# Issuing the two token parities of an expert's first-layer product back to back, into four PSUM banks in turn

## The reference

```python
h = (x_flat @ W_gat).reshape(M, HEADS, NUM_EXPERTS)          # graph attention over 262144 edges
...
agg = jax.ops.segment_sum(msg, dst, num_segments=M).reshape(M, HEADS * NUM_EXPERTS) + b_gat
scores = _layernorm(agg, ln_gamma, ln_beta).reshape(M, HEADS, NUM_EXPERTS).mean(1)
topk_s, topk_i = jax.lax.top_k(scores, TOP_K)
w = jax.nn.softmax(topk_s, axis=-1)
for ei in range(NUM_EXPERTS):
    g = jnp.where(topk_i == ei, w, 0.0).sum(-1)
    hh = jax.nn.gelu(x @ W1[ei] + b1[ei], approximate=False)
    out = out + g[..., None] * (hh @ W2[ei] + b2[ei])
```

## Time and profile before

| | |
|---|---|
| median of 3 runs | 1025.7 us (1022.24 to 1026.14) |
| profiled execution, its own time | 1031.22 us |
| its span, first to last instruction | 1029.5 us |
| busy: TensorE matmul / VectorE / ScalarE / GpSimd | 644.5 / 762.1 / 306.7 / 499.9 us |
| mean granted TensorE clock | 0.748 of full speed |

### The profile page before, as it was taken

The page is one execution under the profiler, slowest core; times in us unless marked ns, Lnnn a source line. Parts: engine busy times, 40 slices in busy tenths (PEclk is TensorE's granted clock), DMA queues, the critical chain, the costliest instruction groups (busy, mean ns, idle before and its releaser), DMA issues.

```text
span 1029.5 us, 15298 instructions
## 1 busy us (share of the span) xinstructions
PE 644.5 (63%) x5984; PEld 331.3 (32%) x5984; DVE 762.1 (74%) x1477; ACT 306.7 (30%) x463; POOL 499.9 (49%) x399
## 2 busy tenths in 40 slices
PE   1501472499788888997787969999999410003421
PEld 1200130133333333333333445555656210002421
DVE  3999887697886877667888779998989831008775
ACT  1510350144554645444444431111111010000015
POOL 3990000017676766650000028888888877756000
PEclk9955875556987977669767969999999855555655
DMA  5010004100000000000000222000000000110001
GB/s 152 0 43 6 8 9 99 24 1 1 1 2 1 1 1 0 0 0 0 2 1 1 82 48 53 6 6 7 6 6 7 7 10 10 10 7 1 3 2 41
DMA packets 22001, 17.08 MB, mean 17 GB/s; under 512 B 13488, under 2 KB 18944, under 8 KB 21168
## 3 DMA queue, kind: packets, MB, share of 16 engines
q1 hardware_dynamic: 15424, 14.02, 5.1%
q0 software_dynamic: 5392, 2.18, 2.6%
q10 hardware_dynamic: 1120, 0.00, 0.1%
HBM read 10.51 MB, written 2.54 MB: 13 GB/s over the span
## 4 chain that ended last, share of the span: by engine, by line
PE 41%; DVE 30%; issue 13%; ACT 4%; SPq 2%; another core or an unknown queue 0%; DMA 0%; DVEq 0%; POOL 0%; ACTq 0%; POOLq 0%
PE psum L615 11%; PE psum L748 10%; DVE mx L1259 7%; PE psum L631 4%; DVE arena L1323 3%; PE psum L646 3%; PE psum L739 3%; PE psum L730 3%; SPq L381 2%; DVE arena L1289 2%; PE psum L598 2%; DVE arena L1030 2%; ACT arena L1004 1%; DVE arena L1026 1%; PE psum L669 1%
## 5 line engine op out<-in xcount | busy, mean ns | idle before, releaser
L493 POOL DMA_INDIRECT work<-node_rows,idx x160 | 257.8, 1611 | 53.1 <-issue 48.5
L1259 DVE TENSOR_REDUCE mx<-psum 128x2 f32<-128x512 f32 x256 | 164.3, 683 | 69.8 <-PE psum L631 67.9
L1323 DVE TENSOR_TENSOR arena<-arena 128x4096 bf16<-128x4096 bf16 (+1 forms) x128 | 182.0, 1486 | 18.1 <-PE psum L748 13.9
L915 ACT ACTIVATE arena<-psum 128x1024 f32<-128x1024 f32 x128 | 129.4, 1024 | 158.4 <-PE psum L646 158.4
L615 PE MATMUL psum<-arena 128*32 128x256 f32 x1024 | 168.3, 486 | 2.3 <-DVE arena L1299 1.4
L470 POOL TENSOR_SCALAR work<-arena,cF 128x184 f32<-128x184 f32 x128 | 93.7, 744 | 129.0 <-DVE arena L1159 73.2
L748 PE MATMUL psum<-arena 128*32 128x128 bf16 x2048 | 131.3, 420 | 4.3 <-DVE arena L1323 3.2
L631 PE MATMUL psum<-arena 32*128 32x256 bf16 x512 | 85.5, 340 | 27.5 <-DVE mx L1259 24.5
L748 PEld LDWEIGHTS psum<-arena 128*32 128x32 bf16 x2048 | 78.2, 149 | 43.6 <-DVE arena L1323 11.6
L615 PEld LDWEIGHTS psum<-arena 128*32 128x32 f32 x1024 | 56.8, 130 | 75.6 <-issue 57.8
L461 POOL COPY arena<-arena 128x160 f32<-128x160 f32 x16 | 5.4, 348 | 136.9 <-DVE arena L1145 91.7
(11 more groups left out here) (290 smaller groups left out, 989.7 us busy)
## 6 DMA issues: line engine op xcount, KB each, us to landing
work<-work SPq DMA_DIRECT2D x48, 64.0 KB, 2.0
work<-node_rows,idx POOLq DMA_INDIRECT x160
arena<-in_L_ffn_edge_index_dram SPq DMA_DIRECT2D x2, 1024.0 KB, 10.6
work<-edge_nodes SPq DMA_DIRECT2D x4, 368.0 KB
digits<-arena SPq DMA_DIRECT2D x1, 1024.0 KB, 4.0
arena<-digits SPq DMA_DIRECT2D x1, 1024.0 KB, 4.9
arena<-in_jpat_dram SPq DMA_DIRECT2D x1, 1024.0 KB, 6.8
out_dram<-work SPq DMA_DIRECT2D x4, 256.0 KB, 2.3
```

The costliest lines, as they stand in the source:

```text
L493: pool.indirect_dma_start(gath[:, l, :], None, tab, bass.IndirectOffsetOnAxis(ap=idx[:, l:l + 1], axis=0)).then_inc(done, 16)
L915: act.activation(pbuf[:, m % 4, :, :, :], ps[:, 2 + 2 * (m % 2):4 + 2 * (m % 2), :].rearrange("p j (k q) -> p j k q", k=U), ACT.Exp).then_ ...
L1259: v.reduce_max(mx[:, h, :], ps[:, h % 2, :].rearrange("p (u k) -> p u k", u=U), AX.X).then_inc(mx_done, 1)
L1323: ins = v.tensor_tensor(oh[:, buf, first:first + n, :], hl2[:, s_, bass.ds(blk * HC, HC)].rearrange("p (j c) -> p j c", j=1).broadcast_to( ...
```

## The change

`up` takes an expert instead of a step. It issues the products of both parities one behind the other, into banks 4 * (e % 2) and 4 * (e % 2) + 1 (so 0, 1, 4 and 5 in turn), and waits once for both. The loop calls it for expert 0 and expert 1 ahead of `down(i, 0)`, for expert 2 ahead of `down(i, 2)` and for expert 3 ahead of `down(i, 4)`; ahead of the other `down`s there is no `up`. The GELU reads the new banks. Nothing else is touched, and every line below L730 has a number higher by one.

```diff
-            def up(i, m):
-                e, u, n = m // 2, m % 2, 8 * i + m
-                if m == 0:
+            def up(i, e):
+                n = 8 * i + 2 * e
+                if e == 0:
                     pe.wait_ge(tns_ready, i + 1)
-                    if isinstance(i, int) and i == 0:
+                    if i == 0:
                         pe.wait_ge(hb_done, 2)
-                if m >= 2 or later(i, 0):
-                    pe.wait_ge(hid_done, n - 1)
-                pe.matmul(ps[:, m % 2, :], w1[C * u:C * u + C, e, :], tns[C * u:C * u + C, :],
-                          start=True, stop=True).then_inc(f1_ready, 1)
+                if n >= 4:
+                    pe.wait_ge(hid_done, n - 2)
+                for u in range(U):
+                    pe.matmul(ps[:, 4 * (e % 2) + u, :], w1[C * u:C * u + C, e, :], tns[C * u:C * u + C, :],
+                              start=True, stop=True).then_inc(f1_ready, 1)
...
                 up(i, 0)
                 for m in range(8):
-                    if m < 7:
-                        up(i, m + 1)
+                    if m % 2 == 0 and m < 6:
+                        up(i, m // 2 + 1)
                     down(i, m)
...
-                act.activation(hid[:, m % 4, :], ps[:, m % 2, :], ACT.Gelu, bias=b1c[:, m // 2:m // 2 + 1]).then_inc(hid_done, 1)
+                act.activation(hid[:, m % 4, :], ps[:, 4 * (m // 2 % 2) + m % 2, :], ACT.Gelu, bias=b1c[:, m // 2:m // 2 + 1]).then_inc(hid_done, 1)
```

## The result

Over 20 executions of each kernel the ratio of the changed kernel's time to that of before is 0.990, with a 95% interval of 0.9853 to 0.9947. On 1025.7 us that is 1015.4 (1010.6 to 1020.3); 1018.6 was forecast, a ratio of 0.993. The change makes the kernel about 1% faster. The medians of all the executions (1026.5 after, 1025.3 before) do not show it, for single ones scatter over 30 us, and the ratios leave out those of a slower state, to which the profiled execution of the changed kernel belongs.

The account below looks back on a forecast made before the run. The end was taken to follow GpSimd's gathers, blocked by VectorE: 0.9 us from the stage plus 6.2 from five more quick gathers gave 7.1, so 1024.1 for the profiled execution and a median of 1018.6 us, range 1015 to 1027.

Parts of the forecast that it names:

- The direction and the path: Whole kernel: faster, because the end follows the gathers, not the stage's end; gathers 92 and 160 come 7.1 us sooner.
- The pair at 1.1 us: TensorE in the stage: a second parity on other array rows is free, so a pair takes about 1.1 us.
- The holes of 0.8 that let a gather in: VectorE idles 0.8 us in steps with a pair, each admitting one quick gather; five more in all, worth 6.2 us.
- Stage: -1 us: The stage's length: 1 us shorter, with bounds of +10 and -10.
- The other way to the same sum: All 160 gathers: 64 blocked at 2.80 and 96 free at 1.25 make 299.2 us, where they now take 306.
- The first chunk: Low clock: a pair takes 2.08 us; the second replaces a 0.8 wait, 1.3 later, partly given back by later steps.
- A chunk's start: Between the counts 3.25 us stand where 2.93 stood, so VectorE's hole grows from 1.84 to about 2.2.
- Slack behind the stage: VectorE's merge after the stage: ready at about 825, needed at 834.7, so 9 us of slack, enough.
- The port: Shared by VectorE and GpSimd: a skill rule implied up to 4.7 us on the stage's end; forecast took no cost.
- Rival 1: The gathers don't profit: holes nearer 0.4 than 0.8 admit none, little beyond the stage's 1 us arrives; chance 0.2.
- Rival 2: Pairs don't overlap: stage up to 10 us later, gathers 9 to 10 sooner, kernel 4 to 10 faster; chance 0.1.
- Rival 3: Slower: the slow products after the stage follow TensorE's place in its instructions and may grow, to 1040 us; chance 0.1.

Follow-up runs that it names:

- less: The changed kernel with 150 gathers in place of 160, the last ten slots of every list left unfetched; ratio to the kernel before 0.9719.
- rows: The changed kernel with each pair made of two experts of one parity, so on the same array rows; ratio to the kernel before 0.9849.
- after5: The changed kernel measured again as it was, in five rounds; ratio to the kernel before 0.9895.
- banks: The kernel before, still one product per step, but with the four PSUM banks of the change; ratio to the kernel before 0.9986.
- tiny: The changed kernel with first-layer products over only 8 of the 512 tokens of a chunk; ratio to the kernel before 0.9964.
- hold: The changed kernel with TensorE's 192 small products waiting for the end of all gathers; ratio to the kernel before 0.9884.
- spread: The changed kernel with `down` of steps 2, 4 and 6 moved between the step's two count blocks; ratio to the kernel before 0.9972.
- pause: The changed kernel with GpSimd waiting between gathers 92 and 93 until the small products are done; span's end 433.4 us after the first one-hot instruction, against 412.2.
- split2: The changed kernel with each 4096-element one-hot instruction cut into two of 2048; 1091 us, the shorter of two runs, against 1032.
- split4: The changed kernel with each 4096-element one-hot instruction cut into four of 1024; ratio to the kernel before 1.1324.
- some: The kernel rows with every fourth block's 4096-element one-hot instruction cut into two of 2048; ratio to the kernel before 0.981.

## Why the prediction was right, point by point

**The direction and the path: right.** The last gather came 9.0 us sooner (7.1 forecast), the turn 9.0 and the end 9.1, and less shows that the end hangs on the gathers. TensorE's 10.8 us less of work were not what counted, as rows shows. The 1024.1 us forecast for the profiled execution came out at 1032.3, because its stage began 10.2 us later; the ratio, 0.990 against 0.993, is what the forecast is to be measured by.

**The pair at 1.1 us: right.** 1.13, and 1.98 without the second set of rows.

**The holes of 0.8 that let a gather in: right.** Measured 0.75 to 0.84, one quick gather in each. The count of five more came out as four, one in each chunk, because the first chunk's first hole did not get longer and took three as before: 4 x 1.25 = 5.0 us instead of 6.2. (The four other traces with the same stage have five or six more.) The reading of the hole of 0.52 stands, although the row at 679.36 in the earlier trace rows is cut off by its window: VectorE goes on there with four instructions, of which 2.33 us is the first.

**The stage: the term that was mis-sized.** "Stage: -1 us" was the working; it measured -3.9 (-3.1 in after5). With the gathers' 5.0 that makes 8.9, against 9.0 measured. So the 7.1 is near the 9.0 partly by luck: the stage's part was 3 us too small and the gathers' part 1.2 too large. Over the five traces with this stage and the two with the one before it, the stage gained 3.5 us and the count 5, so it is the stage's term that was off. The other way to the same sum, 64 blocked at 2.80 and 96 free at 1.25, or 299.2 us, came out at 297.2: the numbers 64 and 96 were right, but the gather that starts behind a hole is held only for what is left of VectorE's instruction, and takes 1.90 to 2.18 us instead of 2.50. Cut at the chunks' first holes, the gain is 0.9 in the first chunk (59.09 to 58.22), 1.05 and 1.17 in the next two and 0.8 in the last. Two things failed:

- *The first chunk.* I put a loss of 1.3 us on the second pair, at the low clock. The two pairs did take 3.79 us, where one took 2.08. But the loss was not there: TensorE no longer idled 0.77 us ahead of `down`, and the granted clock came back sooner. Windows that begin 4.0 and 6.0 us after the first one-hot instruction, first of the kernel before, then of the changed one:

```profile
612.16:614.16 2.00, 2.00 (x16) 1.77 (x19) 1.69 (x2) 0.49 (x2) 1.91 (x1) 0.50 0.87 111
614.16:618.16 4.00, 3.57 (x59) 2.30 (x52) 0.25 (x1) 0.00 (x0) 2.87 (x4) 0.71 0.59 130
```

```profile
622.35:624.35 2.00, 2.00 (x18) 1.43 (x20) 1.69 (x2) 0.38 (x2) 1.90 (x1) 0.80 0.91 118
624.35:628.35 4.00, 3.89 (x64) 2.24 (x56) 0.36 (x1) 0.72 (x2) 2.88 (x4) 1.00 0.70 156
```

  In the first window TensorE is at 1.2 GHz before (0.50) and already mostly at 2.4 after (0.80). `down` took 1.24 instead of 1.97, and the first hole came out at 3.96, no longer than the 4.06 of before. after5 shows the same (0.79, 4.01). The other kernels bear it out: where two full pairs stand ahead of the first `down`, the clock rises 4.1 to 5.5 us after the first one-hot instruction; in before, banks and tiny, where TensorE idles ahead of it (0.77 us, in tiny 0.34), at 8.3 to 8.5. The hole itself is less steady: in less it is 3.29 us, in hold 4.77.

- *A chunk's start.* I put two pairs at 1.11 each and a hole of 2.2. Together they take 1.99, the products stand 2.96 between the counts (671.25 to 674.21) where they stood 2.93, and the hole stayed at 1.8. That is the other 0.2 to 0.4 us in each of the two whole chunks behind the first.

**Slack behind the stage: right.** 9 us forecast for VectorE, 9.45 measured. The end did not turn over to another wait.

**The port.** A quick gather under way when VectorE restarts costs it next to nothing in these traces: in rows one begins at 661.73, VectorE at 661.79, and the eight instructions take 11.31 us as elsewhere; the most is the 2.33 us at 679.36 of the earlier trace rows, where such an instruction takes 2.29 elsewhere. So the rule by which each of the five quick gathers would cost VectorE up to 0.94 us did not come true, and the row that I took held. The other way round the blocking is complete: a gather of 0.94 us mostly takes 2.50 beside 4096-element instructions and 1.43 where they are cut to 2048, and one that starts beside a 4096-element instruction ends 0.82 us behind that instruction's end (the first of all 1.06). The Trainium skill (SBUF — State Buffer, "Who interferes with whom") has such a lock for the whole instruction, but infers that a `tensor_tensor` doesn't hold up the making of DMA descriptors; here `tensor_tensor` with both inputs in SBUF did hold up the issue of gathers, so the inference gives the wrong answer for this case. Whether a gather is held at its descriptors or at the reading of its indices, no run tells.

**The rivals.** Rival 1 did not happen. Rival 2 neither, but rows made it and gave what it said. Rival 3 is refuted by hold. The slow products do not move as a piece, as I had it: they began 11.7 us sooner (234.8 against 246.5), and the last stretch 9.6 sooner. Their end follows the last gather, their beginning the turn and VectorE's merge.

## What to carry to other kernels

Where several engines are near their limit, look for the one that works on alone behind the stage, and ask what blocks it in the stage; here the shorter the stage (tiny, spread), the later the end. Idle time of the blocking engine is worth something only in pieces long enough for the blocked one to start in: a chunk's four or five pauses of 0.2 to 0.43 us gave none, one of 0.8 gave a gather, one of 1.8 two. It need not be as long as the blocked step (0.94 us). A held gather ends 0.82 us behind the end of the 4096-element instruction and the next starts 0.30 later, while VectorE, without a hole, is at its next 4096-element instruction after 0.60 with the short one between; so by these rows a hole of 0.52 us lets one through, and each 1.25 more another: 1.77 for two, so that the holes of 1.80 are only just long enough. Count that currency (quick gathers in the stage) before TensorE's busy time, and shorten the blocking instructions in small doses only, watching the engine that may starve.

## What the runs showed that was not expected

- **TensorE nearly stops beside free-running gathers, once past certain places in its code.** It makes one or two small products per 0.7 to 2.8 us, from there until 6 to 10 us after the last gather's packet; with no gathers in flight the same 192 products take 5.31 us (pause). In split2 and split4 this took over the stage, and went on for some 11 and 21 us after that packet. That the fetching of TensorE's instructions is what is held up fits the packets of the instruction queue at these places, but no run changed the fetching alone: that part stays open, as does why a dose like that of some doesn't start it.
- **Half the length, a third of the blocking.** A gather of 0.94 us loses 1.56 beside a 4096-element instruction (2.50) and 0.49 where it is cut in two (1.43), so a cut block lets two gathers through where one got through. The whole of split2's 73 us is not due to that: most of its gathers began while VectorE stood still.
- **A wait filled with slow work can be free.** The second pair at the low clock cost 1.7 us more of TensorE (3.79 against 2.08) and no time: it filled a wait of 0.77, and the clock rose 4.8 us after the first one-hot instruction, early in `down`, where it had risen at 8.3.
